# Expert-mixture combine: the gathers of tiles 2 and later are issued by GpSimd ahead of the stage border

## What is computed

```
x = x + 0.5 * moe(norm(x))        # stage 0, "moe0"
x = x + retention(norm(x))        # stage 1, "ret"
x = x + 0.5 * moe(norm(x))        # stage 2, "moe0" again
x = x + 0.5 * binarized(norm(x))  # stage 3, "bin"

def moe(x):                       # 32 experts, the 6 best per token
    ...
    y_tok = ye[expert, slot]      # each token's six rows of expert output
    y = sum(y_tok * topk_w)       # weighted sum over the six
    return y + shared(x)
```

## Time and profile before

| what | value |
|---|---|
| median of three runs | 1899.74 us (1897.71 to 1900.02) |
| the profiled execution, its own time | 1901.41 us |
| its span | 1899.6 us |
| TensorE busy | 1580.7 us, 83% |
| VectorE busy | 1427.7 us, 75% |
| ScalarE busy | 1152.8 us, 61% |
| GpSimd busy | 900.3 us, 47% |
| mean granted TensorE clock | 0.906 |

### The profile page before, as it was taken

How to read it: one execution, slowest core, us unless ns; L and a number is a source line. 1 busy time by engine, 2 the same in 40 slices (tenths; PEclk the granted TensorE clock), 3 DMA queues, 4 the chain that set the end, 5 groups by cost and what they waited for, 6 DMA issues and landing times.

```text
span 1899.6 us, 28348 instructions
## 1 busy us (share of the span) xinstructions
PE 1580.7 (83%) x10286; PEld 1282.0 (67%) x10286; DVE 1427.7 (75%) x2995; ACT 1152.8 (61%) x2383; POOL 900.3 (47%) x914
## 2 busy tenths in 40 slices
PE   6899468978997276789888886889999999999775
PEld 4799346866996145578567765667777777777565
DVE  6788568757886666677786756778888888888755
ACT  4588146654883137821872243788888888888542
POOL 0677432003775610030261053166787777878353
PEclk9999688989998587978997987899999999999888
DMA  8798310513994200000003043001000000000243
GB/s 306 220 290 260 94 42 21 184 39 103 284 297 144 84 23 1 1 1 1 1 1 118 19 133 100 15 9 34 17 23 29 23 18 29 23 12 15 91 126 115
DMA packets 87450, 158.89 MB, mean 84 GB/s; under 512 B 13560, under 2 KB 62840, under 8 KB 86264
## 3 DMA queue, kind: packets, MB, share of 16 engines
q1 hardware_dynamic: 72696, 116.96, 18.6%
q0 software_dynamic: 14592, 39.87, 7.4%
HBM read 124.28 MB, written 32.51 MB: 83 GB/s over the span
## 4 chain that ended last, share of the span: by engine, by line
PE 26%; DVE 12%; POOL 7%; ACT 5%; issue 4%; DMA 1%; another core or an unknown queue 0%; POOLq 0%; SPq 0%; DVEq 0%; ACTq 0%
PE ps L79 24%; POOL work L91 3%; DVE work L91 3%; DVE wt L99 3%; PE ps L83 2%; ACT wt L87 2%; DVE ering L91 2%; POOL work_r L91 1%; ACT L87 1%; DVE wt L91 1%; POOL wt_r L91 1%; DVE X L99 1%; DVE H L95 1%; POOL H L145 1%; ACT ering L87 1%
## 5 line engine op out<-in xcount | busy, mean ns | idle before, releaser
L79 PE MATMUL ps<-work_r 128*128 128x256 f32 (+2 forms) x1200 | 243.5, 294 | 5.7 <-ACT work_r L87 1.5
L79 PE MATMUL ps<-wt,work 128*128 128x256 f32 (+1 forms) x1176 | 232.7, 371 | 9.1 <-ACT work L87 8.5
L79 PE MATMUL ps<-H_r,wt_r 128*128 128x512 f32 x576 | 222.7, 431 | 9.8 <-POOL wt_r L91 7.5
L87 ACT ACTIVATE work<-ps 128x512 f32<-128x512 f32 (+5 forms) x339 | 151.6, 477 | 128.8 <-PE ps L79 73.0
L145 POOL DMA_INDIRECT work<-Hd,work x176 | 169.0, 960 | 127.9 <-DVE work L111 84.3
L79 PEld LDWEIGHTS ps<-wt,work 128*128 128x128 f32 (+1 forms) x1176 | 181.0, 201 | 38.9 <-ACT work L87 9.4
L79 PEld LDWEIGHTS ps<-work_r 128*128 128x128 f32 (+1 forms) x1200 | 190.1, 188 | 20.9 <-DVE work_r L91 11.0
L99 DVE SCALAR_TENSOR_TENSOR wt<-ps,wt 128x511 f32<-128x511 f32 (+2 forms) x234 | 174.4, 747 | 22.5 <-ACT wt L87 16.6
L87 ACT ACT_TABLE_LOAD x113 | 145.0, 1283 | 42.6 <-DVE lmv L119 25.2
L91 POOL TENSOR_TENSOR work<-work 128x256 f32<-128x256 f32 (+2 forms) x164 | 162.1, 996 | 6.5 <-ACT work L87 1.3
L91 DVE TENSOR_TENSOR work<-work,ps 48x256 f32<-48x256 f32 (+3 forms) x242 | 128.1, 530 | 49.0 <-PE ps L79 36.8
(11 more groups left out here) (250 smaller groups left out, 4213.3 us busy)
## 6 DMA issues: line engine op xcount, KB each, us to landing
ering<-in_moe_w SPq DMA_DIRECT2D x87, 624.0 KB, 4.8
ye<-work SPq DMA_DIRECT2D x64, 256.0 KB
wt<-in_ssd_wg SPq DMA_DIRECT2D x64, 128.0 KB, 2.2
ye<-work SPq DMA_DIRECT2D x16, 384.0 KB
Hd<-H SPq DMA_DIRECT2D x32, 128.0 KB, 1.7
ye<-early SPq DMA_DIRECT2D x1, 4096.0 KB, 14.6
wt<-in_ssd_wg SPq DMA_DIRECT2D x8, 512.0 KB, 3.6
work<-Hd,work POOLq DMA_INDIRECT x176
```

The source lines that it names most:

```text
L79: self.last = self.e.matmul(o, l, r, start=start, stop=stop, skip_group_check=True)
L87: self.last = self.e.activation(o, a, f, **kw)
```

## The change

At the top of stages 1 and 3 GpSimd now issues the gathers of the "combine" steps before it calls `enter`, and no longer at those steps. Which ones is told by `gathers_ahead(si)`: it walks through `order[si]` and takes every "combine" of a tile above 1 until it meets "fc1". For the retention stage these are tiles 2 to 6 (tile 7's "combine" stands behind the first "fc1" and stays where it was), for the "bin" stage tiles 2 to 7. The waits inside `g_combine` are as they were. No other engine's program changes.

```diff
+        def gathers_ahead(si):
+            todo = []
+            if si and STAGES[si - 1] == "moe0":
+                for s in order[si]:
+                    if s[0] == "fc1":
+                        break
+                    if s[0] == "combine" and s[2] > 1:
+                        todo.append(s)
+            return todo
+
         def g_step(g, s):
             if s[0] == "combine" and s[2] > 1:
-                g_combine(g, *s[1:])
+                if s not in gathers_ahead(s[1] + 1):
+                    g_combine(g, *s[1:])
             elif s[0] == "halve":
                 g_halve(g, *s[1:])
...
             for si, name in enumerate(STAGES):
+                for s in gathers_ahead(si):
+                    g_combine(g, *s[1:])
                 enter(g, si)
                 run[name](g, si)
                 g.mark("end", si)
```

## The result

The changed kernel takes 1901.11 us in the median, the kernel before 1897.99 on the same chip: a ratio of 1.0021, with an interval from 1.0012 to 1.0031. By the medians that is 3.1 us more, by the ratio 4.0. I had forecast 1899.5 and "within 0.2%" as the likeliest case; the size lies inside my range, the direction was given 2 chances in 10. The profiled execution of the changed kernel took 1905.03 us (span 1903.2), 3.6 more than that of before.

A forecast was written before the change was run, and what follows sets the result against it. GpSimd, busy 47%, was taken to matter only where somebody waits for it; VectorE's own work hid the first border. Profiled 1901.41 - 0.24 = 1901.2, less 1.67 to the median, gave 1899.5; range 1887 to 1904.5.

The forecast's parts named there:

- What the gathers do: GpSimd at both borders: same gathers and order, k = 10 near 212.1 and 607.5, k = 19 near 246.4 and 627.0.
- Worth of the first border: Border into stage 1: earlier gathers gain 0, since tile 2's adds at 245.66 wait for nothing gathered; at most 11 us.
- The cost of gathers beside VectorE's last work: Both borders: nine gathers beside VectorE's last adds and sums, cost taken as 0, bounds 0 to +7.1 us.
- the block at 626.41: Tile 2's five VectorE adds in stage 3, 2.84 us beside gathers, the same as without; the basis for charging 0.
- My own bound of +7.1: Both borders: twelve tile 1 adds at 0.93 us, 11.2 us, less 4.1 absorbed by the sums' waits for TensorE.
- The joined row: Second border: rows of 16 and 9 gathers join into 25; 9.3 us lost for 10.5 before, about -1.
- slow stretch: Stage 3, 641.6 to 658.1: VectorE busy only 4.64 of 16.5 us, beginning 19 gathers into a row of 29.
- The first rival: Stage 3's low-busy VectorE stretch goes away: gain 10.5 to 11.2 us, time 1888.7; chance 0.37, gone or mostly gone.
- The second rival: Adds and gathers take turns at both borders: +7.1 us, time 1906.6; chance 0.20, shared with a new slow stretch.
- The third: The change does nothing, not even the 0.24 us at k = 24: 1899.7; within the forecast's 0.43 chance.

The follow-up runs named there:

- the first border alone: Against the kernel before, gathers issued ahead of the border into stage 1 only, not stage 3: 0.9998 where the kernel before takes 1897 to 1907 us.
- the version with the gap: The changed kernel, with gather k = 10 also waiting for VectorE's last shared-expert product: 1892.17 us beside 1898.38 for the kernel before, ratio 0.9960.

## Why the prediction was wrong

**What the gathers do.** Right in their order and length. At border 2 k = 10 starts at 612.14, 1.25 us behind k = 9, as forecast; all lies 4.6 us later than I wrote because stage 2 itself came later. k = 19 starts 0.28 us behind tile 2's first add (forecast 0.1), but at 637.85 instead of 627.0, since the border itself slid.

**Worth of the first border: 0.** Right. Tile 2's adds still run as one block behind it.

**The cost of gathers beside VectorE's last work: taken as 0.** This is the step that failed. I bounded it by turns between adds and gathers, with the block at 626.41 as the nearest row. For the adds the value holds: 2.84 and 2.88 us. I had written that nine gathers run beside "VectorE's last adds and sums", and priced only the adds, because the row I compared with had no instruction that waits for TensorE. The sums do, and their signals were held up: +7.45 us at border 2, +4.8 at border 1 in the profile. My own bound of +7.1 was for both borders together, where the profile has +12.2; that it is near the cost of one of them is chance, since its mechanism was another. The rule of the Trainium skill that I weighed ("SBUF — State Buffer", "Who interferes with whom") did not show here: no add of tile 1 stood behind a gather at the borders in any of these runs. They follow each other by 0.10 us, or wait for their own gather to land.

**The joined row.** I did write down that joining 16 and 9 could start a slow stretch in the row of 25, and put it at 6.3 us, with some 3 us for the next row: 9.3 lost for 10.5. Measured in the profile: 7.45 at border 2 and 4.5 behind it (49.58 us from tile 2's first add to the end, 45.1 on prompt chips), for 11.3 before (56.46). That mechanism was right in kind and its net of -1 was off by less than 2 us. It was wrong to treat it as a property of VectorE in stage 3. It acts on TensorE's and ScalarE's signals too, and so at the first border, where I charged nothing. With the +4.8 there the sum turns.

**The first rival**, the slow stretch gone: half true. Stage 3 became 6.7 us shorter, where it gave 10.5 to 11.2. Against it I had held "20 gathers without a break remain", and these did make tile 6's adds slow. The sign that I had set for it, a busy share above 70% between the adds of tile 4 and those of tile 6, came out at 8.03 of 8.87 us, 91%, without the stretch being gone: it had only moved on to tile 6. **The second rival** had the direction. Its sign came true too, sums that start late without waiting for TensorE by name, but its mechanism is disproved at the borders: the adds there took no turns with the gathers. Both signs were too wide to tell the mechanisms apart. **The third**, nothing changes, holds on prompt chips. Stage 3 changed by 6.75 us, more than the 4 by which I had said the prediction would be wrong.

**What the trace of before could have told.** The word "remote" stood beside waits at both borders: VectorE's instruction ahead of tile 1's adds at 609.69 waited 2.94 us for "remote", and ScalarE's at 209.07 waited 16.53, while the matmuls it needed were over by 202.6. In the earlier trace rows themselves the instruction at 643.09 says "remote"; I read it as waiting for VectorE's own last result, which had ended 1.5 us before, and passed over what that means. I had the name "slow stretch" for one place and didn't look for the same thing elsewhere.

**What stays open.** How signals are held up, and why on some chips only. Whether the first border costs in most unprofiled runs: by the medians the first border alone gave 1.6 us less on a late chip (its row broke by itself) and the second 1.3 us less, by the ratios 0.4 and 2.7, so the two don't add up to the 3.1 us more of both. The joined row at border 1, which the profile of the changed kernel has, could make up the difference; that is not shown, since no run with both borders came to a late chip again, and the +0.21% rests on one comparison. That the border's loss comes from the unbroken row is shown by the version with the gap; that the late chips' whole 41 us and more over the prompt ones comes from late signals is not. The engines' busy times are nearly the same (TensorE 1580.7 and 1577.8 us in the kernel before on a late and the changed one on a prompt chip), the mean granted clock is lower on late chips (0.903 to 0.909 in the profiles, 0.915 to 0.921 on prompt ones), and some 20 of these us lie behind stage 3.

## What to carry over

Work moved into an engine's idle time is free only if nobody needs that idle time; here the gap between two rows of gathers let the other engines' signals through. Keep such rows short, or break them just ahead of the place where another engine's result is awaited; in this kernel a gap of 3 us in the row of 25 turned +0.2% into -0.4% on late chips, each measured in one comparison. When a wait's releaser has no name, compare the end of the instruction that should have released it with the start of the one that waited, everywhere in the trace, before anything is moved.

## What the runs showed of the hardware

On some chips TensorE's semaphore counts arrived up to 9.9 us behind the end of the matmul in the kernel before (199.14 to 209.05) while GpSimd issued gathers without a break, and at both borders within 0.01 to 0.02 us on others. VectorE's own chain then went at 1.40 us an add instead of 0.59 (661.83 to 663.23, against five starts 0.59 us apart in a block of 2.84). Joining nine gathers of 32 bytes per row to a row of 16 was enough (border 2 at 27.35 us, 20.73 before); fills without transfers were nearly harmless (22.42). One and the same kernel differs by 41 to 53 us between the two kinds of chip, ten times what the change was about, so a verdict of a few tenths of a per cent holds for the kind of chip it was measured on.
